# Sums for a batch's first half in the q/k buffer, and the second half's normalisation earlier in the row of cycles

## The chip, the core and the metric

The kernel runs on one core of a Trainium2 chip. The metric is the device time of one execution in microseconds. Five engines work side by side: TensorE (PE, with its weight loads PEld), VectorE (DVE), ScalarE (ACT), GpSimd (POOL) and SyncE (SP), which here only issues DMAs. Each runs its own list of instructions in order, and they wait for each other by semaphores.

## The reference

For x of 8 batches x 1024 rows x 256 columns, all in 32-bit floats:

```
xn = layernorm(x)
# attention on xn, 16 heads of 16
zn = layernorm(xn) * ln_w + ln_b
q, k, v = zn @ Wq.T + bq, zn @ Wk.T + bk, zn @ Wv.T + bv
q, k = rope(q), rope(k)
attn = softmax(q @ k.T / 4) @ v
A = xn + attn @ Wo.T + bo
# experts, 8 of them; each takes the 256 rows of a batch with the highest affinity
affinity = softmax(xn @ gate_w);  rows, gate = top_k(affinity.T, 256)
F = scatter_add(rows, (silu(xs @ Wg) * (xs @ Wu)) @ Wd * gate)   # xs = xn[rows]
result = x + A + F
```

## The kernel before

The program has two parts, one after the other: attention with the router (`attention_part`), then the experts (`expert_part`). The change touches the first alone.

Attention goes batch by batch (`attend(b, nxt, prev)` on each engine). A batch has four groups of four heads; a group goes over two halves of the queries and eight blocks of keys, which makes 64 steps. Two steps are a **cycle**, so a batch is cycles 0 to 31, and group g is cycles 8g to 8g+7. In a step PE multiplies keys by queries into score banks (L745), ACT takes the exponentials (L607, two calls of 128 x 1024 a step, `probs`), and PE weighs the values with them (L759, `o_ps`); DVE copies `o_ps` out every fourth cycle (`copy_o`, L993).

Into these cycles the work of the neighbouring batches is laid. While batch b attends, the next batch is prepared (`nxt`) and the last one is finished (`prev`). On PE a cycle has room for one side job, which writes the one PSUM bank `side`; which job stands in which cycle is a table written by hand (`NEXT_JOBS`, `PREV_JOBS`). PE starts the next job only when DVE has taken the bank's content (semaphore `side_free`). The jobs of interest: cycle 6 `logits`, 7 and 8 the projections of q of the first half (`qk` 0 and 1), 9 a quarter of the output projection of the last batch (`wo`, L685), 10 `qk` 2, 11 the first turning (transpose, L633) of the second half's xn (`x`), 12 `qk` 3 (L649), 13 `x` again, 14 the first turning of z, 15 `wo`, 16 `z`.

The next batch is prepared in two halves of 512 rows, th = 0 and 1. POOL loads x into `xin` (`load_x`, L503). DVE takes the statistics (`norm1`, L812 and L816), POOL the reciprocal deviation (`deviations`, L513 and L515), DVE scales to `xn` and takes the statistics of that (`norm2`), POOL again, DVE scales to `z` (`norm3`, L821). POOL stores xn, adds xn and `bo` to x in place (`base_rows`, L521 and L524) and stores the sums to the output (L528). For q and k of a half, DVE does for s = 0 (q) and s = 1 (k): the four `products` with cosine and sine from `qk` into `rot` (L890), `rotary` back into `qk` (L895, L896), and `split` into a high and a low part (L942, L944), which SP stores. POOL squares the rotated values (L542).

Of the last batch, `o_sums` come back from memory as numerators `num` (SP's `load_num`); DVE inverts the denominators (`invert`, L998), SP stores the reciprocals and reloads them spread out as `rec` (`spread_rec`, L416 and L421: the reload waits until the store has landed), POOL multiplies (`divide`, L548), DVE splits the quotients in four quarters (`quarter_split`, L1007 and L1009), and PE's `wo` jobs project them. `load_num` for the second half of the queries waits until quarters 0 and 1 have been split, since they read the same buffer.

The order on each engine is that of its text: on DVE the ladder of cycle numbers in its `attend`, on POOL and SP a plain list of calls. SP's `attend` also loads the stacks of q and k for the coming group (`load_stack`, eight DMAs, 1.5 MB) once the exponentials of the group before are done, and stores `o_sb` (`store_o`, five DMAs).

Of the kernel before, what the change touches and what calls it, by code (L numbers as in the profile page):

```python
# [112 lines left out]
def attention_part(nc, ctx, g):  # L113
# [154 lines left out]
    SPLIT_CYCLE = (6, 7, 17, 18)  # L268
# [59 lines left out]
    def _(sp):  # L328
# [104 lines left out]
        def attend(b, nxt, prev):  # L433
# [12 lines left out]
            if prev is not None:  # L446
                load_num(prev, 1)
                spread_rec(prev, 1)
# [3 lines left out]
            store_o(b, 1)  # L452
            store_o(b, 2)
# [41 lines left out]
    def _(pool):  # L495
# [5 lines left out]
        def load_x(n, th):  # L501
            hold(pool, base_out, DMA * (2 * n + th))
            pool.dma_start(xin[:, :, :], x[bass.ds(n * S + th * HALF, HALF), :]  # L503
                           .rearrange("(t p) n -> p t n", p=P)).then_inc(x_in, DMA)
# [12 lines left out]
        def base_rows(n, th):  # L517

            out_rows = xn_dram[bass.ds(n * S + th * HALF, HALF), :].rearrange("(t p) n -> p t n", p=P)
            pool.dma_start(out_rows, xn[:, :, :]).then_inc(xn_out, DMA)  # L520
            pool_a.mark(pool.tensor_tensor(xin[:, :, :], xin[:, :, :], xn[:, :, :], ALU.add))  # L521
            pool_a.settle(pool, hold)
            for t in range(HT):
                last = pool.tensor_tensor(xin[:, t, :], xin[:, t, :], bo_sb[:, :], ALU.add)  # L524
            pool_a.mark(last)
            pool_a.settle(pool, hold)
            to = out[bass.ds(n * S + th * HALF, HALF), :].rearrange("(t p) n -> p t n", p=P)
            pool.dma_start(to, xin[:, :, :]).then_inc(base_out, DMA)  # L528
            pool_a.end()
# [279 lines left out]
    def _(dve):  # L809
# [74 lines left out]
        def products(jobs, th, s):  # L884

            cols = slice(th * HALF, (th + 1) * HALF)
# [158 lines left out]
        def attend(b, nxt, prev):  # L1045
            wide = scores_wide(dve, b)
            jobs = jobs_of(b)
            for c in range(CYCLES):
# [19 lines left out]
                if nxt is not None:  # L1068
                    if c == 9:
                        norm1(nxt, 1)  # L1070
                    elif c == 10:
                        norm2(nxt, 1)
                    elif c in (1, 12):
                        norm3(nxt, c // 12)
# [4 lines left out]
                    if c in (11, 21):  # L1079
                        products(jobs, c // 21, 0)  # L1080
                    elif c in (12, 22):
                        rotary(0)
                    elif c in (14, 23):
                        products(jobs, c // 23, 1)
                    elif c in (15, 24):
                        rotary(1)
                    if c in (13, 22):
# [30 lines left out]
        for k, job in enumerate(FIRST_JOBS):  # L1118
# [4 lines left out]
            if job[0] == "qk" and job[2] % 2 == 1:  # L1123
                th, s = job[1], job[2] // 2
                products(first_jobs, th, s)
# [369 lines left out]
```

## Time and profile before

| | |
|---|---|
| time, median of 3 runs | 1924.89 us (1923.93 to 1927.3) |
| profiled execution | 1923.88 us, span 1922.1 us |
| mean granted clock of TensorE | 0.959 |
| PE busy | 1730.4 us, 90% |
| ACT busy | 1185.1 us, 62% |
| DVE busy | 1085.6 us, 56% |
| POOL busy | 662.6 us, 34% |
| exponentials, L607 | 1024 of 1026 ns: 979.3 us busy, 227.2 us idle before them, for PE's scores |
| first and last exponential start | 119.2 and 1283.9 us |

A mean over the span says little here: up to about 1285 us the attention part runs, in which ACT and PE are both nearly full, and then the experts, in which PE is. The batches of the attention part start at about 119, 264, 412, 560, 710, 859, 1006 and 1154 us by the starts of their first exponentials; batches 1 to 6, which have both a next and a last batch in their cycles, take 147 to 150 us.

In the rows, "idle before" in square brackets is the engine's idle time before the instruction and what ended it.

### The profile page before, as it was taken

To read this page: it belongs to the slowest core of one execution; us is meant where nothing else is said; L and a number is where in the kernel's file an instruction comes from. 1 tells how busy PE (TensorE), PEld (TensorE's weight loads), DVE (VectorE), ACT (ScalarE), POOL (GpSimd) and SP (SyncE) were. 2 spreads that over 40 slices of the span, in tenths; PEclk is the share of its full clock that TensorE was granted. 3 is DMA by queue.
4 is the path that set the end of the run, shared out by engine and by line. 5 is a ranking of instruction groups with operands and counts; after the bars stand their busy time and mean duration, and the time that the engine had idled before them with its cause. 6 is when DMAs were issued, how large, how long until landed. Compare 5 with 4: busy or idle time off the path is not lost. (4 is left out here: it accounts for less than half of the span.)

```text
span 1922.1 us, 28864 instructions
## 1 busy us (share of the span) xinstructions
PE 1730.4 (90%) x11240; PEld 1016.0 (53%) x11240; DVE 1085.6 (56%) x1910; ACT 1185.1 (62%) x1390; POOL 662.6 (34%) x599
## 2 busy tenths in 40 slices
PE   2469999999999999999999998872999999999997
PEld 2323434434433444444444343232888888888886
DVE  8846457556656555654655757822545545554543
ACT  0048887887887888788788889961333333333332
POOL 3333123233132133123213311003465565556553
PEclk9669999999999999999999999995999999999999
DMA  3173475476467458447547546423344344344333
GB/s 95 66 157 64 118 151 107 104 165 132 97 162 142 95 141 150 110 125 151 125 119 152 130 98 124 70 71 103 80 91 91 61 97 89 60 96 94 57 60 33
DMA packets 115250, 203.42 MB, mean 106 GB/s; under 512 B 21008, under 2 KB 59280, under 8 KB 115088
## 3 DMA queue, kind: packets, MB, share of 16 engines
q1 hardware_dynamic: 83600, 142.48, 34.1%
q0 software_dynamic: 31488, 58.74, 14.9%
q8 instruction: 106, 1.74, 0.4%
q14 instruction: 56, 0.46, 0.1%
HBM read 116.22 MB, written 84.93 MB: 105 GB/s over the span
## 5 line engine op out<-in xcount | busy, mean ns | idle before, releaser
L607 ACT ACTIVATE probs<-score 128x1024 f32<-128x1024 f32 x1024 | 979.3, 1026 | 227.2 <-PE score L745 227.1
L759 PE MATMUL o_ps<-probs,v_ones 128*32 128x512 f32 x4096 | 505.3, 612 | 0.9 <-ACT probs L607 0.9
L745 PE MATMUL score<-q_stack,k_stack 50*128 50x512 f32 x2048 | 399.8, 460 | 50.1 <-ACT probs L607 40.8
L745 PEld LDWEIGHTS score<-q_stack,k_stack 50*128 50x128 f32 x2048 | 164.9, 187 | 365.0 <-ACT probs L607 298.6
L1302 ACT ACTIVATE silu<-g_ps 128x512 f32<-128x512 f32 x128 | 76.5, 598 | 333.6 <-PE g_ps L1336 333.6
L1262 POOL DMA_INDIRECT out<-y,rows_now x128 | 203.7, 1591 | 206.1 <-DVE y L1415 176.8
L759 PEld LDWEIGHTS o_ps<-probs,v_ones 128*32 128x32 f32 x4096 | 107.8, 110 | 239.4 <-issue 162.6
L542 POOL TENSOR_TENSOR square<-qk 128x512 bf16<-128x512 f32 x64 | 88.2, 1407 | 368.8 <-DVE qk L896 368.8
L1404 DVE TENSOR_TENSOR h<-u_ps,silu 128x512 f32<-128x512 f32 x128 | 88.5, 691 | 209.7 <-PE u_ps L1336 184.8
L1253 POOL DMA_INDIRECT xs<-xn_rows,rows_now x128 | 131.7, 1029 | 38.0 <-issue 29.2
L513 POOL TENSOR_SCALAR ve<-mv 128x4 f32<-128x4 f32 x32 | 7.5, 235 | 307.3 <-DVE mv L816 307.3
L993 DVE COPY o_sb<-o_ps 128x512 f32<-128x512 f32 x64 | 43.9, 685 | 104.8 <-PE o_ps L759 104.8
L1294 ACT CAST h_hi<-h 128x512 fp32r<-128x512 f32 x128 | 78.7, 615 | 33.3 <-DVE h L1404 33.3
L1393 DVE TENSOR_TENSOR h_lo<-h,h_hi 128x512 fp32r<-128x512 f32 x128 | 87.5, 684 | 2.9
L1336 PE MATMUL g_ps<-x_hi,we_hi 128*128 128x512 f32 x256 | 79.9, 393 | 5.1 <-DVE we_lo L1383 5.1
L548 POOL TENSOR_TENSOR num<-num,rec 128x1024 f32<-128x1024 f32 x16 | 38.1, 2382 | 127.8 <-DMA rec<-den_recs 127.5
L1336 PE MATMUL g_ps<-x_hi,we_lo 128*128 128x512 f32 x256 | 79.5, 392 | 0.0
L1336 PE MATMUL g_ps<-x_lo,we_hi 128*128 128x512 f32 x256 | 79.4, 391 | 0.0
L1336 PE MATMUL u_ps<-x_hi,we_hi 128*128 128x512 f32 x256 | 79.2, 391 | 0.0
L1336 PE MATMUL u_ps<-x_hi,we_lo 128*128 128x512 f32 x256 | 79.0, 390 | 0.0
L1336 PE MATMUL u_ps<-x_lo,we_hi 128*128 128x512 f32 x256 | 78.9, 390 | 0.0
L1345 PE MATMUL d_ps<-we_hi,h_hi 128*128 128x256 f32 x256 | 78.2, 306 | 0.7 <-DVE h_lo L1393 0.7
(173 smaller groups left out, 2856.9 us busy)
## 6 DMA issues: line engine op xcount, KB each, us to landing
q_parts<-parts SPq DMA_DIRECT2D x16, 1024.0 KB, 4.3
k_parts<-parts SPq DMA_DIRECT2D x16, 1024.0 KB, 6.9
q_stack<-q_parts SPq DMA_DIRECT2D x64, 256.0 KB, 7.3
k_stack<-k_parts SPq DMA_DIRECT2D x64, 256.0 KB, 9.6
xin<-in_x POOLq DMA_DIRECT2D x16, 512.0 KB, 6.2
xn_rows<-xn POOLq DMA_DIRECT2D x16, 512.0 KB, 4.7
out<-xin POOLq DMA_DIRECT2D x16, 512.0 KB, 3.8
q_stack<-q_parts SPq DMA_DIRECT2D x64, 128.0 KB, 8.2
```

The lines of the kernel that those rows point to most:

```text
L542: last = pool.tensor_tensor(square[i][:, :], qk[:, i, :], qk[:, i, :], ALU.mult)
L607: act.activation(probs[probs_of(s)][:, 2 * i:2 * i + 2, :], score[ring_of(p)][:, :, :], ACT.Exp, scale=SCALE).then_inc(exp_done, 1)
L745: last = pe.matmul(score[ring_of(p)][:, w, :], k_stack[par][rows, i, kt * P:(kt + 1) * P], q_stack[par][rows, i, qh * HALF:(qh + 1) * HALF ...
L759: last = pe.matmul(o_ps[j * KEYS_W:(j + 1) * KEYS_W, :], v_ones[par][:, kt, j, :], probs[probs_of(s)][:, j, :], start=kt == 0, stop=kt == ...
L1253: pool.indirect_dma_start(xs[par][:, t, :], None, xn_dram[:, :], bass.IndirectOffsetOnAxis(ap=rows_now[bp][:, t:t + 1], axis=0))\
L1262: pool.indirect_dma_start(out[:, :], bass.IndirectOffsetOnAxis(ap=rows_now[bp][:, t:t + 1], axis=0), y[par][t][:, :], None, compute_op=ALU ...
L1294: act.copy(h_hi[:, f, :], h[f % 2][:, :]).then_inc(h_high, 1)
L1302: act.activation(silu[f % 2][:, :], g_ps[f % 2][:, :], ACT.Silu).then_inc(silu_done, 1)
L1336: last = pe.matmul(bank[f % 2][:, :], wt[k][w][:, c, f * P:(f + 1) * P], xt[:, c, :], start=i == 0 and c == 0, stop=i == 2 and c == DC - 1)
L1345: last = pe.matmul(rows_ps(t), ht[:, f, t * P:(t + 1) * P], wt[k][DOWN][:, f, :], start=i == 0 and f == 0, stop=i == 2 and f == FC - 1)
L1393: dve.tensor_tensor(h_lo[:, f, :], h[f % 2][:, :], h_hi[:, f, :], ALU.subtract).then_inc(h_split, 1)
L1404: dve.tensor_tensor(h[f % 2][:, :], u_ps[f % 2][:, :], silu[f % 2][:, :], ALU.mult)\
```

## The change

Three things are changed, all in the attention part.

The sums of `base_rows` for th = 0 of the batches prepared in the cycles (n > 0) are written to two of the four planes of `rot`, not over `xin`. The second `load_x` of such a batch no longer waits for the store of these sums, and DVE's first `products` of the batch (th = 0, s = 0) wait for it, since they overwrite `rot`.

In DVE's ladder of cycles `norm1`, `norm2` and `norm3` of the second half stand in cycles 6, 8 and 9, not 9, 10 and 12; the products, rotary and first split of the first half one cycle earlier (10, 11, 12 for q; 13, 14 for k, whose split stays in 15); and the first two quarter splits of the last batch in cycles 7 and 9, not 6 and 7.

On SP, `load_num` and `spread_rec` for the second half of the last batch's queries stand behind the wait for group 0, the stack load of group 2 and the store of `o_sb` of cycle 8, not ahead of them.

```diff
-    SPLIT_CYCLE = (6, 7, 17, 18)
+    SPLIT_CYCLE = (7, 9, 17, 18)
...
             store_o(b, 0)
-            if prev is not None:
-                load_num(prev, 1)
-                spread_rec(prev, 1)
             hold(sp, exp_done, b * PAIRS + GROUP_PAIRS)
             shift_rows(b, 1, wide)
             load_stack(b, 2)
             store_o(b, 1)
+            if prev is not None:
+                load_num(prev, 1)
+                spread_rec(prev, 1)
             store_o(b, 2)
...
         def load_x(n, th):
-            hold(pool, base_out, DMA * (2 * n + th))
+            if th == 0 or n == 0:
+                hold(pool, base_out, DMA * (2 * n + th))
...
         def base_rows(n, th):
 
+            sums = rot[:, 0:2, :].rearrange("p i (t n) -> p (i t) n", n=D) if th == 0 and n > 0 else xin[:, :, :]
...
-            pool_a.mark(pool.tensor_tensor(xin[:, :, :], xin[:, :, :], xn[:, :, :], ALU.add))
+            pool_a.mark(pool.tensor_tensor(sums, xin[:, :, :], xn[:, :, :], ALU.add))
...
-                last = pool.tensor_tensor(xin[:, t, :], xin[:, t, :], bo_sb[:, :], ALU.add)
+                last = pool.tensor_tensor(sums[:, t, :], sums[:, t, :], bo_sb[:, :], ALU.add)
...
-            pool.dma_start(to, xin[:, :, :]).then_inc(base_out, DMA)
+            pool.dma_start(to, sums).then_inc(base_out, DMA)
...
-        def products(jobs, th, s):
-
+        def products(jobs, n, th, s):
+
+            if n > 0 and th == 0 and s == 0:
+                dve.wait_ge(base_out, DMA * (2 * n + 1))
...
-                    if c == 9:
+                    if c == 6:
                         norm1(nxt, 1)
-                    elif c == 10:
+                    elif c == 8:
                         norm2(nxt, 1)
-                    elif c in (1, 12):
-                        norm3(nxt, c // 12)
+                    elif c in (1, 9):
+                        norm3(nxt, c // 9)
...
-                    if c in (11, 21):
-                        products(jobs, c // 21, 0)
-                    elif c in (12, 22):
+                    if c in (10, 21):
+                        products(jobs, nxt, c // 21, 0)
+                    elif c in (11, 22):
                         rotary(0)
-                    elif c in (14, 23):
-                        products(jobs, c // 23, 1)
-                    elif c in (15, 24):
+                    elif c in (13, 23):
+                        products(jobs, nxt, c // 23, 1)
+                    elif c in (14, 24):
                         rotary(1)
-                    if c in (13, 22):
+                    if c in (12, 22):
                         split(nxt, c // 22, 0)
                     elif c in (15, 24):
                         split(nxt, c // 24, 1)
```

On DVE, in the cycles 9 to 11 of batch 1, stood before (`base` is the taking of PE's `wo` job, `qk<-side` that of a projection, `xnT<-side` that of a turning):

```order
L962 TENSOR_TENSOR base<-side,base 128x512 [waits base_in,side_full]
L821 TENSOR_SCALAR xn<-xin,mv,rstd 128x256 [waits xn_out,rstd1_done]
L821 TENSOR_SCALAR xn<-xin,mv,rstd 128x256 x3
L812 BN_STATS stats<-xn 128x6 [waits xn_ready]
L812 BN_STATS stats<-xn 128x6 x3
L816 BN_AGGR mv<-stats 128x2 [waits dve_n]
L816 BN_AGGR mv<-stats 128x2 x3
L881 TENSOR_SCALAR qk<-side,bk_sb 128x512 [waits side_full]
L890 TENSOR_TENSOR rot<-qk,cos_sb 128x512 [waits side_free]
L890 TENSOR_TENSOR rot<-qk,sin_sb 128x512 x2
L890 TENSOR_TENSOR rot<-qk,cos_sb 128x512
L845 COPY xnT<-side 128x512 [waits side_full]
```

And now, in the same cycles (line numbers are those of the changed text):

```order
L1011 CAST at_hi<-num 128x512
L1013 TENSOR_TENSOR at_lo<-num,at_hi 128x512 [waits dve_d]
L823 TENSOR_SCALAR z<-xn,mv,rstd 128x256 [waits rstd2_done]
L823 TENSOR_SCALAR z<-xn,mv,rstd 128x256 x3
L966 TENSOR_TENSOR base<-side,base 128x512 [waits base_in,side_full]
L894 TENSOR_TENSOR rot<-qk,cos_sb 128x512 [waits side_free,base_out]
L894 TENSOR_TENSOR rot<-qk,sin_sb 128x512 x2
L894 TENSOR_TENSOR rot<-qk,cos_sb 128x512
L883 TENSOR_SCALAR qk<-side,bk_sb 128x512 [waits side_full]
L899 TENSOR_TENSOR qk<-rot 128x512 [waits dve_a]
L900 TENSOR_TENSOR qk<-rot 128x512
L847 COPY xnT<-side 128x512 [waits side_full]
```

The products have gone from directly ahead of the copy to `xnT` to a cycle earlier, the scaling to `xn` has gone to cycle 8, and the second quarter split and the scaling to `z` have come in.

On SP, from cycle 4 of batch 1, stood before:

```order
L389 DMA o_sums<-o_sb 4x512 [waits o_copied]
L391 DMA o_sums<-o_sb 16x512 x4
L404 DMA num<-o_sums 128x1x512 [waits at_split]
L404 DMA num<-o_sums 128x1x512
L416 DMA den_recs<-den_rec 128x64 [waits den_done]
L421 DMA rec<-den_recs 128x1x512 [waits rec_out]
L421 DMA rec<-den_recs 128x1x512
L373 COMPARE_AND_BRANCH [waits exp_done]
```

And now, behind the branch and from the second half of the stack load on:

```order
L351 DMA q_stack<-q_parts 32x2x1024
L354 DMA q_stack<-q_parts 16x2x1024
L357 DMA k_stack<-k_parts 16x2x1024
L360 DMA k_stack<-k_parts 32x2x1024
L389 DMA o_sums<-o_sb 4x512 [waits o_copied]
L391 DMA o_sums<-o_sb 16x512 x4
L404 DMA num<-o_sums 128x1x512 [waits at_split]
L404 DMA num<-o_sums 128x1x512
L416 DMA den_recs<-den_rec 128x64 [waits den_done]
L421 DMA rec<-den_recs 128x1x512 [waits rec_out]
L421 DMA rec<-den_recs 128x1x512
L389 DMA o_sums<-o_sb 4x512 [waits o_copied]
```

The numerators and reciprocals have moved behind eight stack loads and five stores.

## Rows read from the trace of the kernel before

**Rows 1.** Timeline of ACT: start, length, instruction, idle before it; one stretch of each batch.

```profile
326.11 1.94 ACT L607 ACTIVATE probs<-score 128x1024 f32<-128x1024 f32 x2 [3.90 <-PE score L745]
...
448.07 1.94 ACT L607 ACTIVATE probs<-score 128x1024 f32<-128x1024 f32 x2 [0.59 <-PE score L745]
...
473.60 1.94 ACT L607 ACTIVATE probs<-score 128x1024 f32<-128x1024 f32 x2 [2.74 <-PE score L745]
...
621.88 1.94 ACT L607 ACTIVATE probs<-score 128x1024 f32<-128x1024 f32 x2 [3.38 <-PE score L745]
...
772.50 1.94 ACT L607 ACTIVATE probs<-score 128x1024 f32<-128x1024 f32 x2 [3.59 <-PE score L745]
...
919.99 1.94 ACT L607 ACTIVATE probs<-score 128x1024 f32<-128x1024 f32 x2 [3.91 <-PE score L745]
```

**Rows 2.** Timeline of PE, batch 2: side jobs of cycles 9, 12 and 14.

```profile
455.43 0.51 PE L685 MATMUL side<-w_hi,at_hi 128*128 128x256 f32 x2
...
471.38 0.74 PE L649 MATMUL side<-zn_hi,w_hi 128*128 128x512 f32 x2 [2.33 <-DVE xnT L845]
...
480.14 0.66 PE L633 MATMUL side<-ident_sb,z 128*128 128x128 f32 x4
```

**Rows 3.** Timeline of DVE, batch 2, cycles 8 to 14.

```profile
450.12 0.69 DVE L993 COPY o_sb<-o_ps 128x512 f32<-128x512 f32 x1 [1.79 <-PE o_ps L759]
...
462.61 2.73 DVE L890 TENSOR_TENSOR rot<-qk,cos_sb 128x512 f32<-128x512 f32 x1
465.26 4.33 DVE L890 TENSOR_TENSOR rot<-qk,sin_sb 128x512 f32<-128x512 f32 x2
469.51 1.22 DVE L890 TENSOR_TENSOR rot<-qk,cos_sb 128x512 f32<-128x512 f32 x1
...
476.39 0.68 DVE L942 CAST parts<-qk 128x1024 fp32r<-128x1024 f32 x1
477.11 1.22 DVE L944 TENSOR_TENSOR parts<-qk,parts 128x1024 fp32r<-128x1024 f32 x1
...
478.85 0.68 DVE L890 TENSOR_TENSOR rot<-qk,cos_sb 128x512 f32<-128x512 f32 x1
```

**Rows 4.** Timeline of POOL, batch 2, cycles 11 and 12.

```profile
462.41 2.38 POOL L548 TENSOR_TENSOR num<-num,rec 128x1024 f32<-128x1024 f32 x1
...
466.63 2.39 POOL L521 TENSOR_TENSOR xin<-xin,xn 128x1024 f32<-128x1024 f32 x1
469.11 3.74 POOL L524 TENSOR_TENSOR xin<-xin,bo_sb 128x256 f32<-128x256 f32 x4
```

**Rows 5.** Timeline of POOL, batch 2, and line L503, all its loads of x.

```profile
437.04 0.78 POOL L503 DMA_DIRECT2D xin<-in_x  x1 [9.87 <-DMA out<-xin]
...
DMA to landing us min/median/max: 4.3/5.0/11.9
```

**Rows 6.** Timeline of SP, batch 2, cycles 6 to 8.

```profile
442.74 1.23 SPq L404 DMA_DIRECT2D num<-o_sums  x2
...
448.92 1.19 SPq L421 DMA_DIRECT2D rec<-den_recs  x2
450.51 0.32 SPq L351 DMA_DIRECT2D q_stack<-q_parts  x1
```

**Rows 7.** Lines L360 from 388 to 394 us, then L411 over the span: issues, landing.

```profile
L360 SPq DMA_DIRECT2D k_stack<-k_parts x2: 423/423/423, 391.5 to 393.4; - x2
...
DMA to landing us min/median/max: 5.8/7.4/9.0
...
DMA to landing us min/median/max: 6.2/12.7/13.3
```

**Rows 8.** Timelines of SP and POOL, batch 4, cycles 0 and 1.

```profile
709.55 1.20 SPq L421 DMA_DIRECT2D rec<-den_recs  x2
...
715.69 2.38 POOL L548 TENSOR_TENSOR num<-num,rec 128x1024 f32<-128x1024 f32 x1 [0.46 <-DMA rec<-den_recs]
```

**Rows 9.** Stretches: cycle 12 of batch 1, 7 of 2. Busy, clock, DMA share, GB/s.

```profile
318.20:326.10 7.90, 5.60 (x30) 2.58 (x22) 7.90 (x11) 3.80 (x5) 6.67 (x6) 0.81 0.52 126
441.74:448.08 6.34, 6.34 (x32) 2.44 (x30) 1.91 (x4) 3.88 (x5) 0.00 (x0) 0.73 0.35 90
```

More of the change, by code:

```diff
@@ L1124, in _ @@
                 th, s = job[1], job[2] // 2
-                products(first_jobs, th, s)
+                products(first_jobs, 0, th, s)
                 rotary(s)
```

## The prediction

> **What bounds the kernel now.** I read the page first (the table above has its numbers): PE is busy 90% of the span, ACT 62%. The change touches only the attention part (to about 1285 us of 1922). There the exponentials of L607 run nearly back to back and PE feeds them, so I read ACT's timeline for gaps. An ordinary gap in a cycle with a projection on PE is 0.57 or 0.58 us. In each of batches 1 to 6 one gap stands out, five of them in [rows 1], the sixth, of batch 6, 2.74 like that of batch 2: 3.90 + 2.74 + 3.38 + 3.59 + 3.91 + 2.74 = 20.26 us, less 6 x 0.58 = **16.8 us**. All are in cycle 12. PE's timeline of batch 2 says why: the projection job of cycle 12 starts at 471.38 after 2.33 us of idleness that DVE's copy to `xnT` (L845) ended [rows 2]. The reader is to see there that PE was not short of work but of the bank `side`, which DVE had not emptied.
>
> DVE was late because of its own four products (L890). Undisturbed such a product takes 0.68 us (at 478.85 in [rows 3]); in cycle 11 the four take 2.73 + 4.33 + 1.22 = 8.3 us instead of 2.7 [rows 3]. They overlap, one for one, with POOL's block of divide (2.38), copy, DMA issue, addition (2.39) and four additions of `bo` [rows 4]: the first ends 0.55 us after the divide, the third 0.6 us after the big addition. An operation of DVE with two inputs in SBUF waits out the POOL operation that is running. The copies out of PSUM in the same stretch are not lengthened.
>
> The Trainium skill, page "SBUF — State Buffer", section "Who interferes with whom", calls the shared port pair an exclusive lock and has a VectorE operation with two SBUF inputs contend with a GpSimd one that reads SBUF. The trace agrees: 0.68 us against 2.73. It speaks against this change, in that a moved product gains nothing if the POOL block moves with it. A shared rate would let each run on at part speed; by it the sum below would lose about a microsecond a batch.
>
> **The change part by part**, with batch 2 as the example and its times of before as marks.
>
> *Sums in `rot`.* As many operations on POOL, of the same size. What goes is the hold of the second load of x: in before the load is issued 9.87 us after the store's issue ended [rows 5]. Now it follows at once, some 9.9 us before 437.04, and its data queue behind that store. Loads of x land in 4.3 to 11.9 us, 5.0 in the middle [rows 5], so x is there at 440 to 442 at the latest. The added wait of DVE on `base_out` before the products of cycle 10 is for a store that landed by 437.04 at the latest, 20 us earlier: nothing.
>
> *norm1 in cycle 6, norm2 in cycle 8, norm3 in cycle 9.* The same 24 DVE operations, 1.8 + 3.2 + 1.6 us. In cycle 6 norm1 takes the place of a quarter split (1.1 us). If x is there by 442 the logits are still taken before PE's next job wants the bank (one job later, 4.7 us after the logits job): 0, else see the rivals. In cycle 8 the copy of `o_ps` starts at 450.12 [rows 3]; behind it norm2 (3.2 us) and the taking of q's second bank (0.75) end at some 454.8, and PE's next side job, L685, starts at 455.43 [rows 2]: hidden by 0.6 us. In cycle 9 the second quarter split (1.1) and norm3 (1.6) stand before the taking of PE's quarter and end it at some 458.2, where PE's next job comes 4.8 us after the last, at 460.2: hidden.
>
> *Products, rotary and split one cycle earlier.* Products in cycle 10 (458.3 to 461.0) and rotary in cycle 11 run with POOL idle, if POOL waits for the sums. Then the wait of 2.33 us before cycle 12 is gone: **-2.2 us a batch** (2.74 - 0.58), and with the clock's share below up to 16.8 us and a little of the gaps behind.
>
> *Numerator and reciprocals later on SP.* This decides where POOL's block goes. SP's rows of before show the numerator loads at 442.74, then the reciprocals' store, their reload at 448.92 and only then the stacks at 450.51 [rows 6]. Now eight stack loads and five stores go first. The exponentials of group 0 end at 448.07 [rows 1], so the stacks start at some 448.6 and, by an undisturbed load of before (last issue 393.4, landed 9.0 later, its first issue seven steps of 0.47 earlier, 12.4 us in all) [rows 7], they land at 461.0. The numerator loads wait for the second quarter split (cycle 9) and are issued at some 456. What is issued behind a stack load lands late: the reload of `base` takes 13.3 us there, 6.2 at best [rows 7]. The numerators and the reciprocals' round trip took 442.74 to 448.92 = 6.2 us in an empty queue. Bounds: from 456.3, beside the stacks, 462.5; from 461.0 and the five stores, behind them, 467.5. I take 466.2, near the late end, since the row of `base` speaks for a queue that keeps its order. From the reload's first issue to the divide it is 715.69 - 709.55 = 6.1 us, where POOL waited for it [rows 8]. So **the divide starts at 472.3** (468.6 to 473.6), in cycle 12, not at 462.41.
>
> The Trainium skill, page "DMA: Bandwidth & Descriptors", section "Queues, rings and completion order", has descriptors of one ring consumed in their order. By it the round trip ends at 466 to 467; were it not so here, at 462.5 and the divide at 468.6. The trace leans to the former (13.3 us against 6.2).
>
> *What the block meets there.* DVE in cycles 12 and 13: the copy of `o_ps` ends at some 469.4, the split (0.69 + 1.22) at 471.3, k's last bank (0.75) at 472.0, the affinities (1.0) at 473.0, then four products and `xnT`, undisturbed done at 476.3. PE wants `xnT` for the z job of cycle 14, at 480.14 in before [rows 2], without the gap of before at 478.0: a slack of 1.7 us. With the divide at 472.3 to 474.7 the first product ends at 475.2; POOL's copy (0.6), the second 476.3; DMA issue and addition (3.2), the third 479.5; one small addition, the fourth 480.7; `xnT` 481.3. That is 3.3 us late. Before a z job, which is short (0.66 us), PE is about 0.9 us ahead of ACT, so ACT loses **+2.4 us a batch**. The stall is not removed but moved, and 0.2 us longer. Further on only ordinary covers: squares still meet the second split, POOL's copy for group 2 is done 9 us before cycle 16.
>
> *The clock.* In cycle 12 of batch 1 the granted clock was 0.81 of 2.4 GHz on the mean, that is, partly at the 1.2 GHz level, with PE busy 5.60 of 7.90 us; in cycle 7 of batch 2 it was 0.73 [rows 9]. Four of the six gaps carry such a stretch: (3.90 + 3.38 + 3.59 + 3.91) / 4 - 2.74 = 0.96 us each. I let three of six keep it, at 0.5 us, since cycles 13 and 14 have slack on PE: 1.5 - 3.8 = -2.3 us. The stretches of cycle 7 stay.
>
> *Batch 0* has no divide; the block meets norm3 and the products with less force than before: -0.3 us.
>
> **Sum:** six batches x (2.4 - 2.2) = +1.2, clock -2.3, batch 0 -0.3: -1.4 us against the profiled execution's 1923.9, that is 1922.5. The median of the three runs is 1.0 above it: 1923.5, rounded to **1923**. The steps "divide at 472.3" and "0.9 us ahead" are the soft ones.
>
> **Rivals.**
> 1. *The stall goes.* The divide starts by 468: it meets the split, not the products. The chain then gives `xnT` at 479.2, ACT loses 0.2 us: 6 x 2.0 = 12, clock 3: 15 us, **1910**. The same if it starts after 474, between the products' second half and rotary, with 0.6 to 1.0 us left: 1914. For it: the round trip alone needs only 6.2 us. Against it: the 13.3 us of `base`.
> 2. *Slower: the block meets both.* If the divide starts just before the split's subtraction (469.4 to 470.1), or at 473 to 474 just before the products, DVE waits for all of the block: `xnT` at 481.5 to 482.2, ACT loses 2.9 on the mean and more, and the clock keeps its share: 6 x (2.9 - 2.2) = 4, and 2 for two more stretches at 1.2 GHz: **1930**. It decides from 0.7 us of the divide's place.
> 3. *x comes late in cycle 6.* DVE waits for x before it takes the logits. From 442.2 on each microsecond is one for PE; 1 us in six batches gives **1929**. For it: the store ahead of it landed only at about 437. Against: 4.3 to 5.0 us is a landing with its fixed part, which now overlaps the store.
> 4. *The clock alone.* The batches shift, and stretches at 1.2 GHz come or go in cycle 7, 1.6 us each (6.34 us [rows 9] against 4.8): two of them, 1920 to 1927.
>
> **How the numbers follow.** The stall moves: 0.44 (faster 0.10, same 0.28, slower 0.06), own range 1918 to 1928. It goes: 0.26, faster. It grows: 0.16, slower. Late x: 0.06 (0.04 slower, 0.02 same). Clock alone: 0.08 (0.03, 0.03, 0.02). Faster 0.39, same 0.33, slower 0.28, with same meaning within 0.2%, 3.8 us, about what a measurement can tell. The range 1907 to 1931 takes in the first two rivals.
>
> **What would show it.** In the changed trace: no wait of PE for L845's counterpart before cycle 12; POOL's divide of the second half with an idle time that the DMA of `rec` ended, some 5.5 us into cycle 12; products of 0.68 us in cycle 10, and stretched ones in cycle 13; a gap on ACT of 2.5 to 3.5 us at cycle 14. A divide before 468 in batch 2's times, or cycle 13 products of 0.68 us, would make the forecast too high; a wait of BN_STATS for x in cycle 6, or stretched split and products both, too low.

## The result, and the profile after

The changed kernel takes **1933.55 us** (median of 12 runs, 1928.65 to 1943.06); the kernel before, run beside it, 1927.70 us (1923.18 to 1931.43). The ratio is **1.0039, with a 95% interval of 1.0022 to 1.0056**: slower by 4 to 11 us. The forecast of 1923 and its range up to 1931 both lie below. The profiled executions are 1933.18 us with a span of 1931.4, against 1923.88 and 1922.1: 9.3 us more in the span, of which 7.4 lie in the attention part (last exponential ends at 1292.3 instead of 1284.9).

PE's waits for DVE, totals over batches 1 to 6 (engine, line, what it waited for: us, times, longest); the kernel before, then the changed one:

```profile
PE side L649 <- DVE xnT L845: 13.9, 6, 2.3
```

```profile
PE side L635 <- DVE xnT L847: 21.2, 6, 4.6
```

The wait ahead of cycle 12 ([rows 2]) is gone. A longer one stands in cycle 14, ahead of the transposition of `z` (L635), which waits for the same kind of copy to `xnT`. In batch 2 the three engines read as follows. PE's timeline, side jobs of cycles 13 and 14, answering to [rows 2]:

```profile
471.77 0.66 PE L635 MATMUL side<-ident_sb,xn 128*128 128x128 f32 x4
478.95 0.66 PE L635 MATMUL side<-ident_sb,z 128*128 128x128 f32 x4 [3.35 <-DVE xnT L847]
```

DVE's timeline, cycles 10 to 14, answering to [rows 3]:

```profile
455.58 0.68 DVE L894 TENSOR_TENSOR rot<-qk,cos_sb 128x512 f32<-128x512 f32 x1
...
466.87 2.64 DVE L946 CAST parts<-qk 128x1024 fp32r<-128x1024 f32 x1
469.54 1.51 DVE L948 TENSOR_TENSOR parts<-qk,parts 128x1024 fp32r<-128x1024 f32 x1
470.98 0.74 DVE L883 TENSOR_SCALAR qk<-side,bk_sb 128x512 f32<-128x512 f32 x1
...
472.05 2.77 DVE L876 TENSOR_SCALAR affinity<-lg_exp,lg_rec 128x8 f32<-128x8 f32 x4
474.74 0.68 DVE L894 TENSOR_TENSOR rot<-qk,cos_sb 128x512 f32<-128x512 f32 x1
475.34 2.35 DVE L894 TENSOR_TENSOR rot<-qk,sin_sb 128x512 f32<-128x512 f32 x2
477.62 0.68 DVE L894 TENSOR_TENSOR rot<-qk,cos_sb 128x512 f32<-128x512 f32 x1
478.22 0.68 DVE L847 COPY xnT<-side 128x512 f32<-128x512 f32 x1
```

POOL's timeline, answering to [rows 4] and [rows 5]:

```profile
424.85 0.76 POOL L504 DMA_DIRECT2D xin<-in_x  x1
...
466.57 2.39 POOL L550 TENSOR_TENSOR num<-num,rec 128x1024 f32<-128x1024 f32 x1 [13.36 <-DMA rec<-den_recs]
...
470.80 2.49 POOL L523 TENSOR_TENSOR xin<-xin,xn 128x1024 f32<-128x1024 f32 x1
473.37 3.78 POOL L526 TENSOR_TENSOR xin<-xin,bo_sb 128x256 f32<-128x256 f32 x4
```

The products of cycle 10 are undisturbed (0.68 us), and x is asked for at 424.85 instead of 437.04. The divide starts at 466.57, where the split of cycle 12 starts, and its idle time was ended by the DMA of `rec`. Here batch 2 runs 2.2 us ahead of its times of before (cycle 12 starts at 464.59 instead of 466.78), so the divide is 2.0 us into cycle 12, which is 468.8 on the marks of before. Over batches 1 to 6 it is 1.3 to 3.0 us into the cycle. Now three kinds of DVE work wait beside the block: the split's CAST (2.64 us, ended 0.55 us behind the divide), the four small scalings of the affinities (2.77 us), and the middle products. Totals over batches 1 to 6 (count, then busy us and mean ns); before, then after:

```profile
L890 DVE TENSOR_TENSOR rot<-qk,sin_sb 128x512 f32<-128x512 f32 x48 | 49.0, 1062 | 0.0
L890 DVE TENSOR_TENSOR rot<-qk,cos_sb 128x512 f32<-128x512 f32 x48 | 48.2, 1005 | 0.2
...
L942 DVE CAST parts<-qk 128x1024 fp32r<-128x1024 f32 x24 | 16.6, 692 | 1.0
L874 DVE TENSOR_SCALAR affinity<-lg_exp,lg_rec 128x8 f32<-128x8 f32 x48 | 7.6, 226 | 0.4
```

```profile
L894 DVE TENSOR_TENSOR rot<-qk,sin_sb 128x512 f32<-128x512 f32 x48 | 36.7, 805 | 0.0
L894 DVE TENSOR_TENSOR rot<-qk,cos_sb 128x512 f32<-128x512 f32 x48 | 33.9, 706 | 0.2
L946 DVE CAST parts<-qk 128x1024 fp32r<-128x1024 f32 x24 | 25.7, 1070 | 0.8
L876 DVE TENSOR_SCALAR affinity<-lg_exp,lg_rec 128x8 f32<-128x8 f32 x48 | 24.2, 570 | 0.4
```

The products got 26.6 us shorter in all; CAST and scalings got 25.7 us longer. The contention was handed on in nearly its full size.

**The account of cycles 12 to 15.** Four cycles that nothing disturbs take 17.12 to 17.15 us, 17.14 in the middle (runs e3, e4 and e7 below). Stretches of the changed kernel, cycles 12 to 15 of batches 2 and 5, then the same of the kernel before, batches 2 and 1 (us; busy time of PE, PEld, DVE, ACT, POOL with counts; granted clock; DMA share; GB/s):

```profile
464.59:486.59 22.00, 18.53 (x122) 7.53 (x114) 17.83 (x21) 15.42 (x17) 16.70 (x13) 0.92 0.27 94
918.50:938.21 19.71, 17.01 (x122) 7.34 (x114) 17.20 (x21) 15.43 (x17) 16.02 (x13) 1.00 0.21 69
```

```profile
466.78:486.33 19.55, 17.22 (x122) 7.42 (x114) 19.38 (x30) 15.31 (x18) 9.78 (x8) 1.00 0.21 68
318.12:339.09 20.97, 18.67 (x122) 8.11 (x114) 19.63 (x30) 15.31 (x18) 10.15 (x8) 0.92 0.28 73
```

At a granted clock of 1.00 the excess over 17.14 is PE's wait to within 0.13 us: 2.41 us with a wait of 2.33 before, 2.57 with a wait of 2.70 after (batch 5). Where the clock was at 1.2 GHz for part of the stretch (0.92 on the mean), 1.4 to 1.6 us come on top. So:

| cycles 12 to 15, batches 1 to 6, us | before | after |
|---|---|---|
| six times 17.14 | 102.8 | 102.8 |
| PE's waits for `xnT` | 13.9 | 21.2 |
| stretches at 1.2 GHz, about 1.45 each | 4: 5.8 | 5: 7.3 |
| remainder | 0.6 | 0.0 |
| in all | 123.1 | 131.3 |

These 8.2 us are the whole loss in the attention part. In each of the five batches the stretch at 1.2 GHz lies behind the new wait. In the other cycles of batches 1 to 6 there are such stretches too (cycle 7 in four batches before and in three after, cycle 18 in one and in three, cycle 0 in one and in one); these cycles took 1.2 us more together. Batch 0 is 2.2 us shorter, of which 1.6 is a stretch in its cycle 18 that did not come again. The two come to about -0.8 together. The last 1.9 us of the span's 9.3 lie behind the attention, where the change moves nothing.

ACT's timeline at cycles 14 and 15 of batch 2 and of batch 5, in place of the gaps in [rows 1]:

```profile
480.13 1.94 ACT L609 ACTIVATE probs<-score 128x1024 f32<-128x1024 f32 x2 [2.72 <-PE score L747]
484.30 1.94 ACT L609 ACTIVATE probs<-score 128x1024 f32<-128x1024 f32 x2 [2.23 <-PE score L747]
...
933.41 1.94 ACT L609 ACTIVATE probs<-score 128x1024 f32<-128x1024 f32 x2 [2.08 <-PE score L747]
935.93 1.94 ACT L609 ACTIVATE probs<-score 128x1024 f32<-128x1024 f32 x2 [0.57 <-PE score L747]
```

In the same place the first gap is 4.58 us in batch 3 and 3.66 in batch 4. In batch 5, at full clock, the wait shows as one long gap and an ordinary one. In batch 2 the second gap is long as well, because PE's weighing between the two took 3.56 us instead of 1.93, at the lower clock:

```profile
480.20 3.56 PE L761 MATMUL o_ps<-probs,v_ones 128*32 128x512 f32 x16
```

### The profile page after: what moved, and what is told of

Its sections match the earlier page's. It is cut to its first block and busy times, and to the rows that moved or that the text cites. A ratio compares the mean times of both kernels' runs of the same rounds, so it can differ in the third digit from the quotient of the medians.

```text
span 1931.4 us, 28871 instructions
## 1 busy us (share of the span) xinstructions
PE 1731.2 (90%) x11240; PEld 1014.6 (53%) x11240; DVE 1085.0 (56%) x1910; ACT 1186.0 (61%) x1390; POOL 663.0 (34%) x599
## 5 line engine op out<-in xcount | busy, mean ns | idle before, releaser
L761 PE MATMUL o_ps<-probs,v_ones 128*32 128x512 f32 x4096 | 511.0, 618 | 0.9 <-ACT probs L609 0.9
```

The lines of the kernel that those rows point to most:

```text
L761: last = pe.matmul(o_ps[j * KEYS_W:(j + 1) * KEYS_W, :], v_ones[par][:, kt, j, :], probs[probs_of(s)][:, j, :], start=kt == 0, stop=kt == ...
```

## The experiments

In what follows "the block" is POOL's divide, copy of `v`, store of `xn`, addition and four additions of `bo`. Ratios are against the kernel before, run on the same chip.

### e1: the order on SP alone put back

```
             store_o(b, 0)
+            if prev is not None:
+                load_num(prev, 1)
+                spread_rec(prev, 1)
             hold(sp, exp_done, b * PAIRS + GROUP_PAIRS)
...
             store_o(b, 1)
-            if prev is not None:
-                load_num(prev, 1)
-                spread_rec(prev, 1)
```

> The changed kernel with SP's order as it was: the numerators and reciprocals of the last batch's second half ahead of group 2's stack load. Theory A (the time went to cycles 13 to 15, where POOL's block of divide and additions meets DVE's split, affinities and products, and TensorE's clock falls behind the wait): the numerator loads wait for the quarter split of cycle 9 all the same, so the divide still starts 1 to 4 us into cycle 12; PE still waits 2.5 to 4 us for xnT before the z job; within 3 us of the changed kernel, about 1933. Theory B (the late place on SP is what costs): the wait goes, 4 to 6 us less than the changed kernel.

Measured: 1937.16 us (1923.51 to 1946.72), ratio 1.0033 (1.0009 to 1.0057). The median is 3.6 us above the changed kernel's, but the ratios are alike (1.0033 and 1.0039), so that the two can't be told apart. The wait before the `z` job is 23.1 us in all, and all six batches show a stretch at 1.2 GHz in cycles 14 and 15, which took 1.4 to 2.9 us on top of the wait. POOL's timeline, batch 2:

```profile
470.15 2.85 POOL L550 TENSOR_TENSOR num<-num,rec 128x1024 f32<-128x1024 f32 x1 [15.01 <-DMA rec<-den_recs]
```

The old order on SP doesn't bring the block back to cycle 11, since the numerator loads still wait for `at_split`, which the moved split gives in cycle 9 (SP stands 21.7 us there and issues them at 455.43). They then hold the stack loads behind them: these were issued from 463.12, where the changed kernel issued its last at 449.10. So the new SP order isn't what moved the block. By SP's wait it is the split's move, though no run puts that back alone; the new order spares the stacks.

### e2: the sums in `rot` alone, x loaded early

The kernel before with `sums`, the guard in `load_x` and the wait in `products`:

```
         def load_x(n, th):
-            hold(pool, base_out, DMA * (2 * n + th))
+            if th == 0 or n == 0:
+                hold(pool, base_out, DMA * (2 * n + th))
...
+            if n > 0 and th == 0 and s == 0:
+                dve.wait_ge(base_out, DMA * (2 * n + 1))
```

> The kernel before, with only the sums in rot, the second load of x at once, and the products' wait for the store; no operation moved in the cycles and SP's order as it was. Theory A: no change against the kernel before, within 2 us, since x was never waited for and the store lands long before the products. Theory C (the second load of x beside the stack load and the base load, or the new wait, costs something): slower by 4 us or more, with a wait on DVE or a later base.

Measured: 1927.22 us, ratio 1.0002 (0.9987 to 1.0016). No change, as theory A has it. The waits of cycle 12 stay at 2.31 to 2.33 us. Neither the other buffer nor the added wait costs or brings anything by itself.

### e6: the moves without the buffer

The changed kernel with the sums in `xin`, the load's wait back and the products' wait gone.

```
-            if th == 0 or n == 0:
-                hold(pool, base_out, DMA * (2 * n + th))
+            hold(pool, base_out, DMA * (2 * n + th))
```

> The changed kernel without the sums in rot: they go over xin again, the second load of x waits for their store, the products wait for nothing. All moves stay. Theory A: x lands about 442.0 in batch 2's times, norm1 ends at 443.9 and the logits are taken just when PE wants the bank: a wait of 0 to 0.6 us in cycle 7, 0 to 4 us more than the changed kernel, 1933 to 1937. Rival F (the early load is what makes the moves affordable): a wait of DVE for x of 3 us or more in cycle 6 and 8 us or more over the changed kernel. Rival C' (the early load costs): faster than the changed kernel by 4 us.

Measured: 1935.27 us, ratio 1.0058 (1.0036 to 1.0080). DVE's timeline in cycle 6 of batch 2:

```profile
437.72 1.41 DVE L813 BATCH_NORM_STATS2 stats<-xin 128x6 f32<-128x256 f32 x4 [2.51 <-DMA xin<-in_x]
...
439.46 0.16 DVE L862 TENSOR_REDUCE lg_max<-side 128x4 f32<-128x32 f32 x1
```

DVE does wait 2.51 us for x, but PE doesn't wait for DVE there, so that even the old load would have served. The buffer is not what the loss comes from, nor would the moves have cost more without it. With e2 this leaves the moves in DVE's row and the block.

### e4: the block without its additions

The changed kernel, for batches 1 to 7 without the additions that form the sums of second halves (the stored base rows are then not the reference's); two copies of 128x4 keep the order.

```
+            if th == 1 and not (isinstance(n, int) and n == 0):
+                pool_a.mark(pool.tensor_copy(ve1[:, :], ve1[:, :]))
...
+            else:
                 pool_a.mark(pool.tensor_tensor(sums, xin[:, :, :], xn[:, :, :], ALU.add))
```

> The changed kernel without POOL's additions for the second half of a batch's rows (the additions of xn and of bo are left out for batches 1 to 7, so those rows of the output lack them; two copies of 128 x 4 keep the count of semaphores). Theory A: the block that DVE meets in cycle 13 is divide and copy alone; affinities take 0.6 and the products 0.68 us each again, PE's wait before the z job is under 0.5 us, six batches x 4 to 4.7 us less: 1905 to 1911. Theory B or C: the additions are not what is waited for, and it stays within 4 us of 1933.

Measured: 1908.03 us, ratio 0.9897 (0.9873 to 0.9921). PE waits nowhere for `xnT`, and cycles 12 to 15 take 17.13 to 17.15 us in each of the six batches. DVE's timeline, batch 2:

```profile
467.33 3.30 DVE L954 TENSOR_TENSOR parts<-qk,parts 128x1024 fp32r<-128x1024 f32 x1
...
471.63 0.63 DVE L882 TENSOR_SCALAR affinity<-lg_exp,lg_rec 128x8 f32<-128x8 f32 x4
472.17 0.68 DVE L900 TENSOR_TENSOR rot<-qk,cos_sb 128x512 f32<-128x512 f32 x1
```

The divide is still there and still meets the split (3.30 us), and that costs nothing. It is the additions that push affinities and products past the point where PE wants `xnT`. Without them the median is 25.5 us lower (1933.55 - 1908.03), near to the 28.5 us that cycles 12 to 15 of the changed kernel have above undisturbed ones.

### e3: the additions ahead of the divide

POOL waits idle for `rec` for 13.36 us in the changed kernel; this puts the additions there.

```
+            if nxt is not None:
+                base_rows(nxt, 1)
             if prev is not None:
...
             if nxt is not None:
-                base_rows(nxt, 1)
                 squares(nxt, 0)
```

> The changed kernel with one thing moved: POOL does the sums of the second half before the divide, in the 13 us in which it waits for the reciprocals in the changed kernel. Theory A: the additions meet z and the products of q in cycles 9 and 10, which have about 4 us to spare before PE wants the bank, and the divide alone meets the split: PE's wait of 3.35 us before the z job falls under 0.8 us and the clock stays up there, 4 us a batch in six batches, about 1908 to 1914. Rival D (the contention only moves again): a wait of 1.5 us or more before cycle 11 or 12, 1925 to 1933.

Measured: **1910.42 us** (1908.66 to 1916.17), ratio **0.9917** (0.9897 to 0.9937): faster than both kernels, with all of the work done. POOL's timeline, DVE's and PE's in batch 2, and the stretch of cycles 12 to 15:

```profile
451.60 2.39 POOL L523 TENSOR_TENSOR xin<-xin,xn 128x1024 f32<-128x1024 f32 x1
...
465.47 2.39 POOL L550 TENSOR_TENSOR num<-num,rec 128x1024 f32<-128x1024 f32 x1 [7.38 <-DMA rec<-den_recs]
```

```profile
450.97 5.45 DVE L824 TENSOR_SCALAR z<-xn,mv,rstd 128x256 f32<-128x256 f32 x4
```

```profile
457.08 0.72 PE L652 MATMUL side<-zn_hi,w_hi 128*128 128x512 f32 x2 [1.38 <-DVE base L967]
```

```profile
463.62:480.75 17.13, 17.09 (x122) 7.41 (x114) 14.51 (x21) 15.31 (x17) 8.29 (x6) 1.00 0.08 26
```

In these four cycles PE is busy for 17.09 of 17.13 us and waits for ACT nowhere, while ACT is busy for 15.31: PE sets their pace. An ordinary gap of ACT in cycle 12, at the place of the long ones of before, is 0.32 us:

```profile
468.01 1.94 ACT L610 ACTIVATE probs<-score 128x1024 f32<-128x1024 f32 x2 [0.32 <-PE score L748]
```

The wait of cycle 14 is gone in all six batches. A smaller one, 1.4 us, has come ahead of the projection of cycle 10, as the additions now meet norm3's four `z` operations, which take 5.45 us instead of 1.38.

### e5: the same reorder without the moves

The kernel before with only the edit of e3.

```
+            if nxt is not None:
+                base_rows(nxt, 1)
             if prev is not None:
...
             if nxt is not None:
-                base_rows(nxt, 1)
                 squares(nxt, 0)
```

> The kernel before with POOL's sums of the second half ahead of the divide, nothing else. There POOL does not wait for the reciprocals, so the order only permutes the same block against the same products. Theory A: four products still take 6 to 8 us, PE still waits 2 to 2.8 us before cycle 12, and the divide now meets z and rotary; within -2 to +6 us of the kernel before, 1924 to 1932. Rival E (it is POOL's order alone that made e3 fast): 10 us or more less.

Measured: 1929.31 us, ratio 1.0015 (1.0000 to 1.0030). PE's waits for DVE over batches 1 to 6:

```profile
PE side L634 <- DVE qk L882: 11.5, 6, 1.9
PE side L650 <- DVE xnT L846: 7.6, 6, 1.3
```

With DVE's work in its old place the block meets products and `z` there. The waits are shorter, 1.3 us ahead of cycle 12 and 1.9 in cycle 13, but longer in sum (19.1 us against 13.9), and the clock fell there in one batch instead of four: cycles 12 to 15 take 123.1 us in all, as before. A stretch at 1.2 GHz in cycle 18 shows in five of batches 1 to 6 instead of one. So neither half of e3 pays alone: the moves give 1.0039, the reorder 1.0015, both together 0.9917.

### e7: e3 with norm3 in cycle 11

```
-                    elif c in (1, 9):
-                        norm3(nxt, c // 9)
+                    elif c in (1, 11):
+                        norm3(nxt, c // 11)
```

> The kernel with the second half's sums ahead of the divide (e3), with the scaling to z moved from cycle 9 to 11. In e3 z took 5.45 us against the additions and PE waited 1.38 us before cycle 10's projection in each of six batches. Theory A: the bank of cycle 9 is taken 5 us sooner, the additions then meet the products in cycle 10 at 1.2 us each, which end some 0.7 us before PE wants the next bank; the 1.4 us go, 6 x 1.45 = 8.7 us: about 1902. Rival D: the wait moves to cycle 11 or 12 (a PE wait over 1 us there), 1906 to 1911.

Measured: 1911.01 us (1903.60 to 1913.89), ratio 0.9911 (0.9889 to 0.9934). The wait of cycle 10 is gone and PE waits for nothing on DVE in batches 1 to 6, and yet the time is that of e3, not the 1902 that its 8.3 us of waits had promised. Where they went is seen in cycle 18. The stretch of it in batch 4, of this kernel and then of e3:

```profile
781.95:787.92 5.97, 5.97 (x34) 1.54 (x36) 1.63 (x3) 3.76 (x5) 0.00 (x0) 0.73 1.04 136
```

```profile
782.76:787.10 4.34, 4.34 (x34) 1.36 (x36) 1.63 (x3) 3.76 (x5) 0.00 (x0) 1.00 1.05 157
```

The same 34 matmuls at a granted clock of 0.73 (partly at 1.2 GHz) instead of 1.00: 1.63 us. In e7 this happens in cycle 18 of five of the batches 1 to 6, in e3 in none; in cycle 7 in five of them against four, and in cycle 0 in two against none. That is 7.7, 1.6 and 3.3 us, some 12.5 together and more than the 8.3 us of waits; this execution (1913.89) is also the longest of its six. Over all six runs the two kernels are even in time, and the mean granted clock is 0.957 in e7 (0.954 to 0.960) and 0.962 in e3 (0.959 to 0.963). PE is busy all through such a stretch of cycle 18, so this is no wait.

### e10: filling for the logits jobs

e7 with two matmuls of 512 columns of no use ahead of each logits job, whose own matmuls are only 8 columns wide.

```
             pe.wait_ge(side_free, jobs.done(("x", th, DC - 1)))
+            for _ in range(2):
+                pe.matmul(bank[:, :], w_hi[WQ][:, 0, 0:P], w_hi[WK][:, :, :].rearrange("p c n -> p (c n)"),
+                          start=True, stop=True)
```

> The kernel with the sums ahead of the divide and z in cycle 11 (e7), in which PE waits for DVE nowhere in cycles 6 to 18, with two more matmuls of 512 columns at the head of each logits job (cycles 6 and 17); the logits overwrite them, so the results are the same. In e7's trace TensorE ran at 1.2 GHz for 3.4 us in cycle 7 of six of batches 0 to 6 and in cycle 18 of five, each 1.5 us. Theory K (these stretches follow the logits job, whose 16 matmuls of 8 columns leave PE nearly idle): most of them go; at 0.24 us a matmul the padding costs 1 us a batch, the stretches gave 2.4: 5 to 14 us less than e7, 1897 to 1906. Rival L (they have nothing to do with the logits job): they stay and it is 3 to 9 us slower than e7, 1914 to 1920.

Measured: 1911.88 us, ratio 0.9911 (0.9891 to 0.9931), between the two expectations. Stretches at 1.2 GHz in cycle 18 of batches 1 to 6: one instead of five; in cycle 7 four instead of five, in cycle 0 none instead of two. Cycle 18 of batch 4, then its cycle 7:

```profile
783.41:787.75 4.34, 4.34 (x34) 1.36 (x36) 1.63 (x3) 3.76 (x5) 0.00 (x0) 1.00 1.05 158
...
731.71:738.04 6.33, 6.33 (x32) 2.24 (x30) 2.38 (x9) 3.88 (x4) 1.36 (x2) 0.76 0.01 4
```

Filling costs 0.47 us in each of its cycles (5.16 instead of 4.68 or 4.69), so some 7 us in all, and that uses up more than half of what the missing stretches give (11 us by the same count as above). The mean granted clock over its six runs is 0.960, between e7 and e3. That fits theory K for cycle 18, but doesn't prove it: there is one trace of each, and e3, without filling, has no stretch in cycle 18 either. For cycle 7 it speaks against theory K.

### e8: the affinities in cycle 11

The changed kernel, with the small scalings out of the block's way.

```
-                    elif c in (13, 21):
+                    elif c in (11, 21):
                         affinities(nxt, c // 21)
```

> The changed kernel with the affinities of the first half in cycle 11 instead of 13, where POOL is idle. In the changed kernel their four small scalings took 2.77 instead of 0.63 us, and stood ahead of the stretched products. Theory A (whatever DVE does first waits out the addition): the affinities take 0.63 us, the first product or two wait in their place; xnT is at most 1 us sooner; 0 to 6 us less than the changed kernel, 1927 to 1933. Rival G (the affinities' own wait is what made PE late): PE's wait before the z job falls by 2 us or more, 12 us or more less.

Measured: 1922.28 us, ratio 0.9979 (0.9962 to 0.9995), 11 us below the changed kernel: more than the 0 to 6 us that theory A had allowed, and less than rival G asked for (12 us, and 2 us of each wait). The divide stands as far into cycle 12 as in the changed kernel, 2.2 us on the mean in both. DVE's timeline of batch 2, and PE's wait over the six batches:

```profile
472.60 3.55 DVE L894 TENSOR_TENSOR rot<-qk,cos_sb 128x512 f32<-128x512 f32 x1
```

```profile
PE side L635 <- DVE xnT L847: 14.3, 6, 3.6
```

The first product now waits where the scalings did (3.55 us), and still the waits fall from 21.2 to 14.3 us: -6.9. The clock fell behind them in two batches instead of five: 3 x 1.45 = -4.4. The sum is -11.3, the medians' difference 11.3 and that of the profiled spans 9.1. So the scalings, 128x8 numbers each, cost a good microsecond of wait a batch; that the clock gave the rest is read from one trace of each.

### e9: the reciprocals' round trip early

The changed kernel with `spread_rec` back ahead of the stack load and `load_num` behind it.

```
             store_o(b, 0)
+            if prev is not None:
+                spread_rec(prev, 1)
...
                 load_num(prev, 1)
-                spread_rec(prev, 1)
```

> The changed kernel with the reciprocals' round trip back in its old place on SP and only the numerator loads behind the stack load and the store. Theory A (the place of POOL's block decides): in batch 2's times of the changed kernel the divide starts at 460 to 463 instead of 466.6, two to five us before cycle 12, the second addition ends by 468, so it meets the split at most and the products of cycle 13 take 0.68 us each; PE's wait of 3.35 us before the z job falls under 0.8, six batches x 4: 1905 to 1913. Rival H (with the stack load pushed back to 450 and the numerators behind it, the divide comes no earlier than 465): as the changed kernel or worse, 1930 to 1937.

Measured: 1923.35 us, ratio 0.9972 (0.9955 to 0.9989), between the two expectations, for a reason that makes it the best witness of the account: in this one trace the block lands in two places. Where the divide starts 1.8 to 2.9 us ahead of cycle 12 (batches 2, 3 and 4) there is little or no wait; where it starts 1.5 to 3.5 us into it (1, 5 and 6), 2.9 to 3.9 us. Cycles 12 to 15 of batches 2 and 1:

```profile
469.57:486.70 17.13, 17.13 (x122) 7.41 (x114) 14.25 (x21) 15.32 (x18) 13.21 (x11) 1.00 0.25 84
...
318.54:341.79 23.25, 19.34 (x122) 8.01 (x114) 18.39 (x21) 15.42 (x18) 17.52 (x13) 0.85 0.32 111
```

| batch of e9 | divide against start of cycle 12, us | PE's wait before the `z` job | cycles 12 to 15 |
|---|---|---|---|
| 2 | -2.93 | 0 | 17.13 |
| 3 | -2.42 | 0.27 | 17.29 |
| 4 | -1.84 | 0.78 | 17.89 |
| 6 | 1.51 | 2.90 | 21.53 |
| 5 | 3.17 | 3.92 | 22.47 |
| 1 | 3.47 | 3.91 | 23.25 |

A wait of 0.78 us costs 0.75, and one of 0.27 costs 0.15. There is next to no slack, some 0.1 us, between PE and ACT at that job. Why the numerators, which the divide now waits for, land at such different times was not tried; in batch 2 they were issued at 458.47, right behind stack loads and stores.

## Why the prediction was wrong

**What held.** The wait ahead of cycle 12 came from the block and went with the products' move. The block moved to cycles 12 and 13, with the DMA of `rec` as what POOL waits for. DVE waits for x twice, 1.68 us in batch 1 and 0.21 in batch 3, which PE doesn't feel, and the covers of cycles 6, 8, 9 and 10 hold: PE waits for DVE nowhere in them for the norms or the products. `rot` and the products' wait are free (e2). It isn't in these steps that the forecast failed.

**"PE is about 0.9 us ahead of ACT": the step that failed.** By it a wait of 3.3 us was to cost ACT 2.4. The waits measure 3.53 on the mean (21.2 / 6), near to the 3.3, and each costs its whole length: 2.57 for 2.70 in batch 5, 0.75 for 0.78 in e9. PE isn't ahead of ACT there, since it sets the pace of these cycles itself (e3). The trace of before could have said so: in its four cycles of 19.55 us PE is busy for 17.22, and the other 2.33 are the wait in [rows 2]. That wait lengthened them by 2.41 (19.55 - 17.14), more than the 2.16 that I read off ACT's gap. The gap of 2.74 holds the whole loss, but an ordinary one at its place is 0.32 us (e3, 468.01), not the 0.58 that I took off. The term "6 x (2.4 - 2.2) = +1.2" should have been 21.2 - 13.9, which is 6 x (3.53 - 2.32) = **+7.3**. Of the 6.1 us between, 5.4 are the slack that isn't there.

**"Clock -2.3": wrong sign.** I let four stretches of 0.96 us go with the old wait and gave the new one three of 0.5, since I held that cycles 13 and 14 have slack. Five of six batches show a stretch at 1.2 GHz behind the new wait, at 1.45 us each and not 0.5, 7.3 us against 5.8 before: **+1.5**. What the runs show is that the fall goes with the wait and not with cycle 12: in the 24 batches (1 to 6) of e3, e4, e7 and e10 PE doesn't wait in cycles 12 to 15, and none has one there. Not every wait brings one: two of six batches before and one after have none.

Together: 7.3 + 1.5 against 1.2 - 2.3 is 9.9 of the 10.7 us between the forecast's -1.4 and the profiled +9.3. The rest is small: -0.6 (the remainder in the table), -0.5 (batch 0 and the stretches elsewhere, -0.8 against the forecast's -0.3), +1.9 behind the attention. The second rival, "the block meets both", has the right mechanism and side; its price, 6 us, was too low for the same two reasons.

**"The divide at 472.3": mis-sized, and made up for by luck.** On the marks of before it started at 468.8, which is 3.5 us too early and the early end of my range (468.6); the other 2.2 us to the measured 466.57 are the lead of the whole batch. The numerator loads were issued at 453.49 and the reload at 461.17, 7.7 us later, where an empty queue took 6.2 [rows 6] and I had allowed some 10, since eight stack loads lay ahead. From the reload to the divide it was 5.4 us instead of 6.1. SP's timeline:

```profile
449.10 0.42 SPq L360 DMA_DIRECT2D k_stack<-k_parts  x1
...
453.49 1.48 SPq L404 DMA_DIRECT2D num<-o_sums  x2
455.01 0.46 SPq L416 DMA_DIRECT2D den_recs<-den_rec  x1
...
461.17 1.19 SPq L421 DMA_DIRECT2D rec<-den_recs  x2
```

I had taken the queue to keep its order, from the 13.3 us of `base` [rows 7], and named for it what the Trainium skill, "DMA: Bandwidth & Descriptors", "Queues, rings and completion order", says of descriptors consumed in ring order. The trace neither bears that out nor refutes it: the last stack load landed 9.3 us behind its issue, at 458.4, and the store of the reciprocals at some 461.1, behind it. What was mis-sized is the time behind the stacks: from their landing to the reload it was 2.8 us, where I had put 5.2 (461.0 to 466.2).

My first rival let the stall go for a divide by 468, which is 1.2 us into cycle 12. Its bound was too late: batch 5, with 1.31, still waited 2.70 us, since the block's additions meet what comes behind the split. In e9 the stall is all but gone at -1.84 and earlier.

**"Affinities 1.0": a cover that was missed.** I gave contention to operations with two inputs alone. The split's CAST reads one tensor, and each scaling one with a factor to a row. They took 2.64 and 2.77 us beside the block, where undisturbed the CAST takes 0.68 (e4 and e8) and the four scalings 0.63 (e4). Without the scalings' loss the early divide would have left more room; e8 puts it at 6.9 us of waits. The Trainium skill, "SBUF — State Buffer", "Who interferes with whom", does list copy, cast and tensor_scalar among what can take the shared ports; the trace agrees, and I had used only its half on two inputs. That the wait came out near to the forecast one, 3.35 us in batch 2 against 3.3, is luck: the divide came 3.5 us too early, and CAST and scalings, which I had left as they were, were stretched in place of some of the products.

**The median.** The forecast stood on three runs of before with 1924.89; twelve give 1927.70. That is 2.8 us of the 10.5 between 1923 and 1933.55.

**Open.** Why the clock falls in cycles 7 and 18 in some batches and not in others e10 leaves open, and so does the fall behind a wait: in e2 four of six batches show it in cycles 12 and 13, as before, but not the same four. What moves the landing of the numerators in e9 wasn't tried.

## What to carry to other kernels

Work moved out of one collision should be followed until the other engine's block has found its new place: here the block was moved along by a wait on a round trip, and met the next row of work, while its engine stood idle for 13 us beforehand; filling that idle time (e3) turned 0.4% slower into 0.8% faster. Price a wait of the feeding engine by its busy time in the whole stretch of cycles and by the stretch's length against an undisturbed one, not by a gap on the engine that is fed less some other gap. And expect that part of a gain can be lost again in clock: e7 removed 8.3 us of waits and kept none of it, at a mean granted clock of 0.957 against 0.962.

## What the runs showed of the hardware

- Small operations of one input wait out a POOL operation too: four scalings of 128x8 took 2.77 us instead of 0.63, a CAST 2.64 instead of 0.68, norm3's four `z` 5.45 instead of 1.38. The taking of a bank out of PSUM did not: 0.74 us at 470.98, inside the addition that ran from 470.80 to 473.29.
- A cycle with the granted clock partly at 1.2 GHz took 1.2 to 1.7 us longer in cycles 0, 7 and 18, the latter two with PE busy throughout. In cycles 12 to 15 of before and after it came behind a wait of PE, in 4 of 6 batches before and 5 of 6 after, and cost 1.4 to 1.6 us; in e1 up to 2.9.
- The store of the reciprocals to their reload took 6.2 us with eight stack loads ahead of it on the same queue, the last landed 3.4 us behind the store's issue (455.01 to 461.17), and 4.8 us with none (e1, 456.70 to 461.52). From the reload to the divide it was 5.4 us and, in e1, with the stack loads issued right behind, 8.6. In this pair, batch 2 of each, the loads behind cost the small transfer more than those ahead.
- In one execution of e9 the same block started at -2.9 to +3.5 us against its cycle. A placement that depends on when a DMA lands can be good in one batch and bad in the next.
